# A two-layer gated cross-attention network on one core: expert tiles beside the last routing, token rows ahead of weights, the next attention's first group in the same block, and the last layer's end groups in halves

## What is computed

```python
x = x + tanh(g_xattn[0]) * attention0(layernorm(x), ctx, ctx)   # 16 heads of 8 channels, with an output product
x = x + tanh(g_ffn[0])   * experts(layernorm(x))                # router: the best 2 of 8 experts, gates sum to 1
x = x + tanh(g_xattn[1]) * attention1(layernorm(x), ctx, ctx)   # one head, tanh on the values, key mask
x = x + tanh(g_ffn[1])   * quantized_ffn(layernorm(x))          # 8-bit rounding with scales of the whole tensor
```

## Time and profile before

| | us |
|---|---|
| median of 3 runs (lowest to highest) | 962.2 (956.12 to 962.82) |
| the profiled execution, its own time | 955.83 |
| its span, first to last instruction | 954.1 |
| TensorE's share of the span busy | 77% |
| VectorE, ScalarE, GpSimd | 78%, 64%, 63% |
| mean granted TensorE clock (share of full speed) | 0.881 |

### The profile page before, as it was taken

How to read it: one execution, slowest core, us unless ns; L and a number is a source line. 1 busy time by engine, 2 the same in 40 slices (tenths; PEclk the granted TensorE clock), 3 DMA queues, 4 the chain that set the end, 5 groups by cost and what they waited for, 6 DMA issues and landing times. The chain is left out here.

```text
span 954.1 us, 19490 instructions
## 1 busy us (share of the span) xinstructions
PE 733.8 (77%) x6612; PEld 569.6 (60%) x6612; DVE 748.8 (78%) x1759; ACT 613.4 (64%) x1206; POOL 602.9 (63%) x608
## 2 busy tenths in 40 slices
PE   5898889999899997305899999999954888264255
PEld 3666667667677776204778888887842667132054
DVE  4899978888878885513868887887848899499998
ACT  4666657767676763203767777777753877499393
POOL 3574467878787788661546667676664882597400
PEclk9999979999999998556989999999985999567556
DMA  9325422222223212134757767776719333000023
GB/s 251 97 79 109 106 70 102 82 105 93 105 98 109 96 46 99 64 121 179 248 215 262 250 229 256 247 243 247 252 59 343 120 104 95 14 0 1 1 67 111
DMA packets 88625, 128.20 MB, mean 134 GB/s; under 512 B 19392, under 2 KB 62352, under 8 KB 82512
## 3 DMA queue, kind: packets, MB, share of 16 engines
q1 hardware_dynamic: 77952, 106.55, 34.0%
q0 software_dynamic: 9120, 18.91, 5.8%
q10 hardware_dynamic: 1456, 1.51, 0.5%
HBM read 82.66 MB, written 44.18 MB: 133 GB/s over the span
## 5 line engine op out<-in xcount | busy, mean ns | idle before, releaser
L1506 POOL DMA_INDIRECT m_results<-e_y,e_to x156 | 165.4, 1060 | 99.7 <-ACT e_y L1568 61.7
L344 POOL TENSOR_TENSOR a_probs<-a_probs,a_top 128x1024 f32<-128x1024 f32 x64 | 122.0, 1907 | 73.6 <-DVE a_top L1003 72.9
L378 POOL DMA_INDIRECT m_tokens_to<-r_rows,r_place x128 | 130.5, 1019 | 37.1 <-issue 32.4
L1544 ACT ACTIVATE e_h<-e_bank,e_bias 128x512 f32<-128x512 f32 x156 | 108.5, 696 | 45.3 <-PE e_bank L1646 39.3
L1758 DVE TENSOR_TENSOR e_hp<-e_h,e_hp 128x512 fp32r<-128x512 f32 x156 | 110.7, 710 | 5.4
L453 ACT ACTIVATE a_probs_t<-a_ps_pt 128x512 f32<-128x512 f32 x128 | 69.4, 591 | 69.8 <-PE a_ps_pt L699 69.7
L1756 DVE CAST e_hp<-e_h 128x512 fp32r<-128x512 f32 x156 | 76.1, 488 | 43.6 <-ACT e_h L1544 37.0
L956 DVE TENSOR_TENSOR a_probs<-a_ps_s,a_mask 128x1024 f32<-128x1024 f32 x64 | 77.9, 1217 | 11.2 <-PE a_ps_s L551 10.8
L675 PEld LDWEIGHTS a_ps_o<-a_vals,a_probs_t 128*64 128x64 f32 x2048 | 67.0, 141 | 21.0 <-issue 20.4
L1288 DVE TENSOR_REDUCE d_hpeak<-d_hid 128x1 f32<-128x2048 f32 (+1 forms) x36 | 70.6, 2039 | 9.8 <-ACT d_hid L1207 9.8
L1003 DVE TENSOR_REDUCE a_top<-a_probs 128x16 f32<-128x1024 f32 x64 | 77.1, 1205 | 0.1
(11 more groups left out here) (293 smaller groups left out, 1933.8 us busy)
## 6 DMA issues: line engine op xcount, KB each, us to landing
e_weights<-m_weights_to SPq DMA_DIRECT2D x39, 1024.0 KB
e_rows<-m_tokens_to SPq DMA_DIRECT2D x39, 264.0 KB, 3.9
m_weights_to<-r_parts SPq DMA_DIRECT2D x8, 1024.0 KB, 4.7
c_two<-m_results SPq DMA_DIRECT2D x5, 1024.0 KB, 11.1
a_ctx_in<-in_ctx_dram SPq DMA_DIRECT2D x17, 256.0 KB, 3.1
m_keys_t<-n_keys SPq DMA_DIRECT2D x16, 256.0 KB
m_values<-n_values SPq DMA_DIRECT2D x16, 256.0 KB
c_keys_t<-m_keys_t SPq DMA_DIRECT2D x16, 256.0 KB, 2.7
```

The source lines that it names most:

```text
L344: pool.tensor_tensor(probs[:, j], probs[:, j], top[:, j].unsqueeze(2).broadcast_to([P, HEADS, SEQ]), ALU.subtract).then_inc(shifted, 1)
L378: pool.indirect_dma_start(tokens_to, bass.IndirectOffsetOnAxis(ap=place[:, k, q:q + 1], axis=0), rows[:, c % RING, q % CT, k, :], None).th ...
L1506: pool.indirect_dma_start(results, bass.IndirectOffsetOnAxis(ap=to[:, v, r:r + 1], axis=0), y[:, v, r], None).then_inc(sent[v], 16)
L1544: act.activation(h[:, c], ps_h[c][:], ACT.Gelu_apprx_tanh, bias=bias[:, n % ROWS, c:c + 1]).then_inc(h_sb, 1)
```

## The change

**Order of the experts.** `layer0` and the expert half of block 2 are one function, `layer0_and_experts`. The scattered rows of the first five chunks (EARLY_CHUNKS = 5) are enough for 13 full tiles whatever the routing: `early_tables` makes tables for these after chunk 4's places, in group 13's steps, and `late_ends` and `late_tables` those of the other 26 in tile steps 5 and 6. Tiles begin in step 64 of the attention (TAIL), as soon as the last scores are done and chunk 4's rows have landed; the last four steps of the attention and the routing of chunks 6 and 7 are written out by hand between the parts of the first tiles. The table look-up is 6 instructions over (tile, expert) pairs in place of 24.

**Buffers.** PSUM holds 8 banks, all of which block 1 uses, so the tiles take banks over as they come free. Down products have one bank for tiles 0 to 9 (ONE_BANK = 10) and two after that, where they had two. Rows, gelu results, `q_t`, `spread` and the first loads of results share one tensor, `room`. The results have 8 buffers (YRING) and not 2, in the space of `a_probs`.

**Queues.** GpSimd's order is fixed: from chunk 6 on, scatters and returns together are limited to 5 indirect DMAs (PACE) per tile by a wait on the up products. The cast of the row numbers moves to VectorE (`take_numbers`). For tiles 3 to 12 SyncE loads rows two tiles ahead of weights (ROWS_AHEAD = 2) and then in the old order; the ten loads before tile 6 are gone, and their like stands after tile 38 or in the next block.

```diff
+        def beside_products():
+            nonlocal paced
+            if paced >= 0 and paced % PACE == 0:
+                pool.wait_ge(h_ps, min(paced // PACE + 1, ETILES - 1) * CHUNKS + 1)
+            if paced >= 0:
+                paced += 1
...
+        for n in range(SETS, SETS + ROWS_AHEAD):
+            load_rows(n)
+        for n in range(SETS, EARLY):
+            if n + ROWS_AHEAD < EARLY:
+                load_rows(n + ROWS_AHEAD)
...
+            load_expert(n)
+        sp.wait_ge(tables_ready, 4)
+        sp.wait_ge(padded, 16 * (2 * SPARE + EXPERTS))
+        for c in range(NCH - RING, NCH):
+            sp.wait_ge(sent[c % RING], rows_sent(c))
+        for n in range(EARLY, ETILES):
+            load_rows(n)
+            load_expert(n)
```

```diff
+        dve.wait_ge(two_in[0], 16)
+        dve.tensor_tensor(two[:, 0, :, 0], two[:, 0, :, 0], two[:, 0, :, 1], ALU.add).then_inc(f_summed, 1)
...
+        for k in range(QUAD):
+            dve.tensor_scalar(xn[:, 0, k], x_sb[:, k], f_mv[:, k, 0:1], f_rstd[:, k:k + 1],
+                              ALU.subtract, ALU.mult).then_inc(f_xn_ready, 1)
```

```diff
+        for i in range(2):
+            pe.wait_ge(hq_ready, LAST + 2 + i)
+            products(LAST, (ps_y[LAST % 2], ps_h[0])[i], (2 * i, 2 * i + 1))
```

More of the change, by code:

```diff
@@ L519, in _ @@
                     queries(n)
-                if j == 2 and there(s, SUPERS):
+                if j == 2:
                     if s == 0:
@@ L645, in _ @@
                 t = s * QUAD + j
-                if there(t, TILES) and j % 2 == 0:
+                if j % 2 == 0:
                     if j == 0:
@@ L713, in _ @@
+                if j == 0 and n < SUPERS:
                     if t - 2 >= 0:
@@ new lines, in part @@
+        def part(t, c):
+            n, m, last = t + 1, t + 2, t - 1
+            if there(n, ETILES):
+                up(n, c)
+            if there(t, ETILES):
+                down(t, c)
+            if c == 0:
+                if there(m, ETILES):
+                    expert_transposes(m)
+                if there(last, ETILES):
+                    result_transposes(last)
+        t = TAIL
+        turn_free(t)
+        pe.wait_ge(placed, PLACE_OPS * (NCH - 3) + 2)
+        router(SUPERS - 3)
@@ new lines, in _ @@
+        heads_product(t)
+        pe.wait_ge(x2t_sb, SUPERS - 2)
+        probs_transposes(t)
+        pe.wait_ge(k1_sb, SUPERS)
+        part(-2, 0)
+        heads_transpose(t)
+        t = TAIL + 1
+        turn_free(t)
+        pe.wait_ge(l_sb, SUPERS - 2)
+        counts(NCH - 2)
+        heads_product(t)
+        probs_transposes(t)
+        pe.wait_ge(s_sb, TILES)
+        part(-1, 0)
+        heads_transpose(t)
+        for c in range(1, CHUNKS):
+            part(-1, c)
+        t = TAIL + 2
```

1743 lines of the change are left out of this document (1013 added, 730 removed).

## The result

The changed kernel takes 912.5 us (median of 4 runs, 907.88 to 912.83) against 960.98 for the kernel before in the same runs: a ratio of 0.9492, 95% interval 0.9444 to 0.9539. It was forecast at 907 against 962.2, a ratio of 0.943, just outside that interval, with 886 to 932 as the range. The profiled execution took 912.67 us, its span is 911.0.

A forecast was written before the change was run, and what follows sets the result against it. TensorE was taken as nearly idle from 395 to 442 us and full mid-experts. 954.1 - 60.4 + 1.3 + 2.5 + 2.5 - 1.0 = 899.0 of span, 900.7 executed, times 1.0067 gives 907; range 886 to 932.

The forecast's parts named there:

- the early tables: Group 13's attention steps: 18 small VectorE instructions, 3.6 us, of which 2.5 counted; bounds 0 and 3.6.
- Part 1: Start of the experts: first up product at 379, tile 0's up products done by 393, 61.4 us earlier.
- rival D: First tiles still wait for the last rows, or run at 1.2 GHz, about 10 us; 0.06 with cases towards A.
- Part 2: Tiles from tile 0's up products to the last product: 247.9 us before, -7.3, +8 and +2.5, ending at 644.1.
- The 7.3 us of the ten loads: Tiles 3 to 8: time lost with ten loads queued before tile 6, now saved; -3.6 if only half goes.
- the interleaving: Tile steps shared with routing, late tables and attention: +8 us, bounds 0 and 32.
- one bank: Tiles 0 to 9: down products wait for an eviction, 0.25 us each, +2.5; bounds 0 and 15.
- Part 3: GpSimd's 188 indirect DMAs at 1.36 us end at 644; last return 8.4 us after the last product, at 652.5.
- Rival C: GpSimd becomes the bound beside the tiles, from 1.72 us per DMA on; span 966 at 1.78; chance 0.04.
- Part 4: Last return to next attention's first exponential: 21.35 us as before, plus 1.3 for the barrier.
- Parts 5 and 6: Attention: weights' work +2.5 us and early tables +2.5; last layer: last group's products in halves, -1.0.
- The halves: Last layer: the last group's first half runs while the second is clamped, -1.0 us; bounds -2 and +0.5.

The follow-up runs named there:

- b1_loads_last: The kernel before with its ten loads for the attention moved from before tile 6 to behind tile 38; 950.54 us, ratio to before 0.991.
- o1_one_bank: The changed kernel with one bank for down products in all 39 tiles, not in ten; 979.68 us on a slower chip, ratio to before 0.995.
- e3_pool_waits: The changed kernel with root and mask row first, and GpSimd's sums held until the first maxima; 970.19 us on a slower chip, ratio to before 0.991.
- e1_root_first: The changed kernel with group 1's root moved ahead of the queries' eviction on ScalarE; 967.68 us on a slower chip, ratio to before 0.988.
- e2_mask_first: The changed kernel with group 1's root first and group 0's mask row loaded ahead of results; 968.03 us on a slower chip, ratio to before 0.986.
- f1_best: The changed kernel with group 1's root first, mask row first and no rows ahead of weights; 975.50 us on a slower chip, ratio to before 0.988.
- e1_again: The changed kernel with only group 1's root moved first, timed again; 973.20 us on a slower chip, ratio to before 0.988.
- r0_rows: The changed kernel with no rows loaded ahead of weights (ROWS_AHEAD = 0 in place of 2); 910.00 us, ratio to before 0.948.
- w0_no_prep: The changed kernel without the preparation of layer 1's feed-forward weights inside the attention; 968.89 us on a slower chip, ratio to before 0.988.
- p8_pace: The changed kernel with eight indirect DMAs allowed per tile in place of five; 989.50 us on a slower chip, ratio to before 1.003.

## Why the prediction was right, and where it was off

The sign and the place of the gain were right, and the gain is mostly the one forecast: the tiles in the idle stretch. The number came out nearer than its parts deserve, as the last paragraph of this section shows. By the prediction's steps, in us:

| step | forecast | measured | off |
|---|---|---|---|
| first up product (with 2.5 more for the early tables) | 381.5 | 379.0 | -2.5 |
| weights of tile 3 issued | 14 later | 14.5 later | +0.5 |
| last product | 251.1 later | 254.3 later | +3.2 |
| last return | 8.4 later | 10.0 later | +1.6 |
| first exponential | 22.6 later | 29.2 later | +6.5 |
| attention's end | 82.8 later | 85.2 later | +2.4 |
| span's end | 138.5 later | 138.8 later | +0.3 |
| span | 899.0 | 911.0 | +12.0 |

**Part 1** held to a microsecond: the start is set by step 64's transposes, and what precedes the first product on VectorE was read off the last chunk's rows. The early tables cost nothing that is seen. The low clock that rival D priced at 10 us did not come in the first tiles: the granted clock is 1.00 from 379 to 401 us and 0.84 from 401 to 412.

**Part 2.** The 7.3 us of the ten loads are confirmed by b1_loads_last. The shared steps were mis-sized: +13.6 us from tile 3 to 13 over the steady pace, against 8 for the interleaving and 2.5 for one bank. One bank is nearly free in the later tiles (o1_one_bank); if it is in the first ten too, the interleaving costs some 13. The prediction counted VectorE's and ScalarE's work there and let TensorE's own pass. Over these ten tiles (columns as in the first table of the section on the result):

```profile
393.50:471.52 78.02, 70.34 (x346) 56.40 (x345) 61.53 (x153) 54.59 (x108) 50.76 (x51) 0.98 0.71 233
...
440.79 1.47 SPq L211 DMA_DIRECT2D m_tokens_to<-r_pad  x2
448.84 0.50 PE L964 MATMUL a_ps_s<-e_xt,e_weights 128*128 128x512 f32 x1 [2.01 <-DMA e_weights<-m_weights_to]
```

TensorE is busy 70.34 us, where ten steady tiles of before have 63.9 (191.62 in 30, from 493.87 to 687.16). So 6.4 of the 13.6 are work of TensorE's own, the attention's and the routing's products. It waits 3.3 us for evictions on ScalarE, 2.7 for weights, and 1.3 for nothing that the profile shows. The queue, then, is the smaller part. And scatters, rows and weights are not alone in keeping the DMA engines busy 0.90 from 443.30 on: eight stores of padding, 264 KB each, stand in SyncE's queue from 440.79 to 460.0, six of them between 443 and 463, 1.6 of the 6.2 MB moved then. Before, the like were issued from 402.9 to 407.3, where TensorE was idle, and the prediction does not name them. It gave steps above 7 us past tile 6 as a sign of being wrong. That sign is there for tiles 6 to 10, 37.54 us or 7.5 each, and gone from tile 11 on. One step, tile 2's from 401.14 to 411.82, takes 10.7 us, where the prediction allowed 3 above 6.44.

**Part 3.** In the middle of the tiles GpSimd is as full as TensorE, as was worked out: 1.35 us per DMA (1.045 and 0.30), 1.36 forecast. It does not bound the tiles. When the last product ends, eight returns are still to come, from 648.00 on at 1.26 us: 10.1, and that is the 10.0 measured in place of 8.4. They are not there because GpSimd was behind:

```profile
641.44 1.13 ACT L702 ACTIVATE a_probs<-a_ps_pt,room 128x128 f32<-128x128 f32 x4
642.55 1.20 POOL L477 DMA_INDIRECT m_results<-a_probs,e_to  x1 [0.59 <-ACT a_probs L702]
645.77 1.14 ACT L702 ACTIVATE a_probs<-a_ps_pt,room 128x128 f32<-128x128 f32 x4 [0.81 <-PE a_ps_pt L993]
```

GpSimd still waits for the copies of the third last tile (641.44). Those of the last two follow 4.33 and 3.53 us behind one another (645.77 and 649.30), as no next tile's products stand between, and four returns take 5.1. The forecast's floor of 7.7 took the last tile's four returns behind its copies and left out those of the tile ahead of it.

**Rival C**, GpSimd as the bound, did not come about on this chip: 1.35 us per DMA with its issue, where 1.72 was needed. The Trainium skill's rule on the shared port ("SBUF — State Buffer", section "SBUF: two separate sides"), by which a DMA that GpSimd issues takes some 3100 ns beside a VectorE copy and some 620 alone, is not borne out: 1045 ns at the mean beside 312 splits and the routing. But a port shared by the two would fit the other finding: VectorE's own tensor_tensor goes from 0.69 to 1.4 to 1.8 us beside GpSimd's tensor_tensor, in the changed kernel and in e3_pool_waits. The runs show the lengthening and what goes with it, not the port.

**Part 4** is the step that failed. The prediction took everything behind the barrier as the same and added 1.3 us for it (1.8 measured, to TensorE's first transpose). In fact the code's order on ScalarE had changed: the root of group 1, which stood ahead of the queries' eviction, now stands behind it. VectorE loses 2.38 us there, and since GpSimd's additions begin in that time, it meets them with three instructions that ran alone before. Moving the one line back takes 4.4 us off this stage. The order of the two kernels' ScalarE queues would have shown it; it was read for TensorE, GpSimd and SyncE only. A part of it is given back in the attention, 1.8 us by the means (84.8 in the five with the old place, 86.6 in e1_root_first, e2_mask_first, f1_best and e1_again), so the net by the means of such profiles is 2.7 us (113.8 and 111.1). These are from different chips, r0_rows with the old place has the 111.8 of f1_best and e1_again nearly to the tenth, and no time shows the net.

**Parts 5 and 6.** Attention +4.9 with 2.5 forecast. w0_no_prep gives 3.0 where the weights' work stands and 0.6 over the whole, so 2.5 is neither confirmed nor refuted; the rest is another cause (below). The halves gave 0.7 of span, 1.1 up to the last result, with 1.0 forecast; they were not tried by themselves.

**The median.** The 12 us are on the executions' own times: 900.7 against 912.67. The prediction then multiplied by 1.0067, since the profile of before lay below its median. The profile of after lies at its median, so this factor, 6 us that answer to nothing in the changed kernel, hid about half of the miss. That the median came within 5.5 us of 907 is luck to that extent.

## What to carry to other kernels

When work is moved from one block to another, print each engine's queue of both kernels around the seam, not only of the engines that the change speaks of: one small instruction placed behind a wait cost more than the barrier that it came with. Look for the cheap part in a large change and try it alone: here ten loads in a queue held 8.3 of 48 us. And a limit that spaces one engine's DMAs is worth trying by itself: with 8 a tile in place of 5 the kernel was the slowest of the four on its chip, for a cause that stays open.

## What the runs showed that was not expected

**TensorE's clock inside the attention.** In the changed kernel the granted clock falls to 0.50, the 1.2 GHz level, for some 6 us in the middle of the attention, at about 738, beside two waits of TensorE (1.56 us ahead of 736.39, 0.98 ahead of 738.53; columns as in the first table of the section on the result):

```profile
739.00:744.00 5.00, 5.00 (x19) 3.90 (x18) 2.50 (x10) 1.97 (x7) 3.56 (x4) 0.50 0.29 86
```

Two groups' exponentials are 6.74 us apart there (738.23 and 744.97), and 3.99 in r0_rows, where the clock is 1.00 in the same step. The mean clock from the first to the last exponential is 0.91, and 0.96 before. That can be where the attention's other 2 us went, but it is not shown: r0_rows has as low a mean clock, 0.91, from dips elsewhere, and takes 84.5 us, and no run varied the clock alone.

**Chips differ in more than speed.** On both slower chips the profile has waits of ScalarE and VectorE that end "remote", in the tiles and the first attention, and GpSimd has some too, but for p8_pace (4.5 to 11 us in all); in all six profiles from the other chips there is none. In e1_again ScalarE's main row (us in total, times, longest) is

```profile
ACT room L683 <- remote: 20.8, 9, 4.0
```

and VectorE's "remote" waits add up to 33.6 us. With PACE = 8 they are 47 and 54.2 us. The longest come with GpSimd's runs of indirect DMAs, but the cause stays open: the limit of 8 is the one run that varied this, no run of the changed kernel or profile of the one before is from such a chip, and so it is not known how much of the changed kernel's gain is left there. The variants of it gained 0.5 to 1.5% there, p8_pace nothing, where the changed kernel and r0_rows gained 5% on the other chips.
